# Gather targets of a graph-network kernel: sixteen copies of the prefix rows, and other rows for empty slots

## The reference, cut to what matters

```
h = layernorm(x), clipped at 0
h = h @ W.T + b
_, topk_idx = top_k(adj, 32)           # the lowest index wins among equal values
x = x + max(h[topk_idx], axis=1)
```

## Time and profile before

| | |
|---|---|
| median of three runs | 3695.63 us (3692.3 to 3698.97) |
| span of the profiled execution | 3738.5 us |
| TensorE, VectorE, GpSimd, ScalarE busy | 90%, 70%, 69%, 43% |
| the chain that ended last | TensorE 65%, VectorE 21%, issue 5%, GpSimd 4% |
| GpSimd products L498 | 1024 of 1307 ns |
| gathers L506 | 980, about 1 us each |

### The profile page before, as it was taken

The page is one execution under the profiler, slowest core; times in us unless marked ns, Lnnn a source line. Parts: engine busy times, 40 slices in busy tenths (PEclk is TensorE's granted clock), DMA queues, the critical chain, the costliest instruction groups (busy, mean ns, idle before and its releaser), DMA issues.

```text
span 3738.5 us, 76487 instructions
## 1 busy us (share of the span) xinstructions
PE 3378.0 (90%) x29444; PEld 3342.4 (89%) x29444; DVE 2622.0 (70%) x5491; ACT 1607.0 (43%) x3554; POOL 2592.6 (69%) x2448
## 2 busy tenths in 40 slices
PE   6999999999999999999999999942899898989894
PEld 6999999999999999999999999942888898989894
DVE  6788888788788788211177664647787878878767
ACT  6777887787787786222122211221111111112114
POOL 3998998998998997000487856647888878777500
PEclk9999999999999999999999999975999999999997
DMA  6999999999999999788888888842788887878781
GB/s 217 397 396 367 388 385 352 386 389 352 386 391 351 384 376 388 276 291 296 290 322 319 299 294 311 293 154 77 269 286 291 300 308 284 295 280 308 259 293 57
DMA packets 401324, 1155.22 MB, mean 309 GB/s; under 512 B 36717, under 2 KB 56110, under 8 KB 401006
## 3 DMA queue, kind: packets, MB, share of 16 engines
q1 hardware_dynamic: 360096, 1082.21, 78.4%
q0 software_dynamic: 31360, 64.29, 5.5%
q10 hardware_dynamic: 9550, 4.69, 0.4%
HBM read 874.19 MB, written 276.86 MB: 308 GB/s over the span
## 4 chain that ended last, share of the span: by engine, by line
PE 65%; DVE 21%; issue 5%; POOL 4%; ACT 2%; DMA 1%; another core or an unknown queue 1%; DVEq 1%; POOLq 0%; SPq 0%; ACTq 0%
PE psU L667 18%; PE psT L751 18%; PE psT L655 9%; PE psT L783 8%; PE psU L751 6%; DVE agg L1684 4%; DVE HT L1680 3%; PE psU L783 3%; DVE D L1473 2%; POOL D L498 2%; POOL D L506 2%; DVE GR L1843 1%; DVE W L1684 1%; DMA adj_turned<-ATS 1%
## 5 line engine op out<-in xcount | busy, mean ns | idle before, releaser
L498 POOL TENSOR_TENSOR D<-D,iota 128x512 f32<-128x512 f32 x1024 | 1307.3, 1307 | 115.9 <-ACT D L910 97.6
L667 PE MATMUL psU<-HB,ATS 128*128 128x129 f32 x8192 | 1007.1, 276 | 28.4 <-ACT ATS L903 26.3
L667 PEld LDWEIGHTS psU<-HB,ATS 128*128 128x128 f32 x8192 | 961.1, 193 | 33.3 <-ACT ATS L903 28.6
L783 PE MATMUL psT<-ATS,PIECES 128*128 128x129 f32 x6144 | 804.7, 281 | 172.7 <-ACT ATS L1069 79.3
L783 PEld LDWEIGHTS psT<-ATS,PIECES 128*128 128x128 f32 x6144 | 751.5, 196 | 186.3 <-issue 143.8
L1473 DVE MAX8 D<-D 128x8 f32<-128x512 f32 x1024 | 644.2, 683 | 259.7 <-POOL D L498 251.9
L751 PE MATMUL psT<-GR,PIECES 128*128 128x129 f32 x6144 | 780.7, 276 | 20.1 <-issue 19.3
L751 PEld LDWEIGHTS psT<-GR,PIECES 128*128 128x128 f32 x6144 | 733.2, 192 | 24.9 <-issue 24.2
L506 POOL DMA_INDIRECT D<-h_table,idx_own x624 | 628.4, 1007 | 170.4 <-issue 150.3
L903 ACT ACTIVATE ATS<-psT 128x512 f32<-128x512 f32 x1024 | 555.9, 596 | 270.4 <-PE psT L655 177.1
L910 ACT ACTIVATE D<-PIECES 128x1024 f32<-128x1024 f32 x512 | 544.1, 1063 | 0.0
(11 more groups left out here) (410 smaller groups left out, 2896.9 us busy)
## 6 DMA issues: line engine op xcount, KB each, us to landing
PIECES<-adj_turned SPq DMA_DIRECT2D x512, 1024.0 KB
PIECES<-in_adj SPq DMA_DIRECT2D x256, 1024.0 KB
adj_turned<-ATS SPq DMA_DIRECT2D x512, 512.0 KB, 8.2
D<-h_table,idx_own POOLq DMA_INDIRECT x624
h_table<-HB ACTq DMA_DIRECT2D x8, 512.0 KB, 6.6
D<-h_table,idx_pool POOLq DMA_INDIRECT x215
out_x<-X SPq DMA_DIRECT2D x3, 1024.0 KB, 5.1
ATS<-h_table,idx_pool POOLq DMA_INDIRECT x117
```

The lines of the kernel that those rows point to most:

```text
L498: pool.tensor_tensor(key, key, iota[:, :], ALU.mult).then_inc(keyed, 1)
L667: last = nc.tensor.matmul(sum4(r), AT[K % NAT][:, b * GROUP + r * P:b * GROUP + (r + 1) * P], HB[:, j, :], start=(j == 0 and r % 2 == 0), ...
L783: last = nc.tensor.matmul(acc(h, r), block_of(slot, b, r), Hc[par][:, jj, :], start=(jj == 0 and opens(r)), stop=(jj == CT - 1 and closes(r)))
```

## The change

- The table begins with 16 copies of the 65 prefix rows, 1040 rows in place of 65 (`COPIES`, `BASE`). One DMA writes them all. Each partition uses the copy of its number divided by 8: `lane[:, 2:3]` holds 65 times that, and it is added wherever k was used.
- An empty own slot repeats the first neighbour of its line of eight (near or far). Only where the row has none there does it hold the prefix row as before.
- An empty shared slot reads row 1039 + 15 times the partition's number for near lists, 1039 + 47 times it for far lists. The mask takes its value out as before.
- VectorE builds `lane[:, 2:3]` ahead of the pass, in 15 comparisons that each add to it. Each pick gets two more instructions, and three of its instructions get one more operand. The steps of a staged list (L1534 to L1551) stay as many.

```diff
+COPIES = 16
+    NEAR_STEP, FAR_STEP = 15, 47
-    table = nc.dram_tensor("h_table", (HEAD + N, P), fp32).ap()
+    BASE = COPIES * HEAD
+    table = nc.dram_tensor("h_table", (BASE + N, P), fp32).ap()
+    heads_v = table[0:BASE, :].rearrange("(c p) f -> p c f", p=HEAD)
...
-            pool.iota(lane[:, :], [[0, 1]], base=0, channel_multiplier=1,
+            pool.iota(lane[:, 0:1], [[0, 1]], base=0, channel_multiplier=NEAR_STEP,
+                      allow_small_or_imprecise_dtypes=True).then_inc(ident_ready, 1)
+            pool.iota(lane[:, 1:2], [[0, 1]], base=0, channel_multiplier=FAR_STEP,
...
-                    nc.scalar.dma_start(table[0:HEAD, :], pfxn[:, :]).then_inc(head_stored, 16)
+                    nc.scalar.dma_start(heads_v, pfxn[:, :].unsqueeze(1).to_broadcast([HEAD, COPIES, P])).then_inc(head_stored, 16)
...
+                lists, fills = [a.rearrange("p r (l k) -> p (r l) k", k=8) for a in (top, topd)]
...
+                pk.mark(v.scalar_tensor_tensor(fills, lists, 0.0, lists[:, :, 0:1].to_broadcast([P, 2 * TPG, 8]),
+                                               ALU.is_equal, ALU.mult))
                 pk.mark(v.tensor_copy(POOLN[:, g, :], pooln[:, 0:NEAR_POOL]))
...
+                pk.mark(v.tensor_tensor(lists, lists, fills, ALU.add))
                 pk.mark(v.tensor_tensor(zcum, zcum, sp[:, 2, :].unsqueeze(2).to_broadcast([P, TPG, PREFIX]), ALU.is_lt))
...
-                pk.mark(v.tensor_copy(IDXN[:, ts, 0], sp[:, 3, :]))
+                pk.mark(v.tensor_scalar(IDXN[:, ts, 0], sp[:, 3, :], lane[:, 2:3], None, ALU.add))
...
-                    pk.mark(v.tensor_tensor(into, topd[:, :, to:to + count],
-                                            sp[:, 3, :].unsqueeze(2).to_broadcast([P, TPG, count]), ALU.add))
+                    pk.mark(v.scalar_tensor_tensor(into, topd[:, :, to:to + count], lane[:, 2:3],
+                                                   sp[:, 3, :].unsqueeze(2).to_broadcast([P, TPG, count]),
+                                                   ALU.add, ALU.add))
...
-                link(v.scalar_tensor_tensor(key, empty, lane[:, 0:1], key, ALU.mult, ALU.add))
+                link(v.scalar_tensor_tensor(key, empty, lane[:, 0:1] if near_list else lane[:, 1:2], key, ALU.mult, ALU.add))
...
             dve.wait_ge(pick_constants, 4)
+            link(v.memset(lane[:, 2:3], 0.0))
+            for k in range(1, COPIES):
+                link(v.scalar_tensor_tensor(lane[:, 2:3], lane[:, 0:1], float(NEAR_STEP * k * (P // COPIES)) - 0.5,
+                                            lane[:, 2:3], ALU.is_gt, ALU.add))
+            link(v.tensor_scalar(lane[:, 2:3], lane[:, 2:3], float(HEAD), None, ALU.mult))
+            link(v.tensor_scalar(row_base, row_base, lane[:, 2:3], None, ALU.add))
             link(v.tensor_copy(basep, cbase))
```

More of the change, by code:

```diff
@@ L109, in build @@
     HEAD = PREFIX + 1
-    table = nc.dram_tensor("h_table", (HEAD + N, P), fp32).ap()
-    near_table = table[0:HEAD + NEAR * PIECE, :]
-    early_table = table[0:HEAD + LATE * SGW, :]
-    table_v = table[HEAD:HEAD + N, :].rearrange("(t p) f -> p t f", p=P)
+    BASE = COPIES * HEAD
+    table = nc.dram_tensor("h_table", (BASE + N, P), fp32).ap()
+    near_table = table[0:BASE + NEAR * PIECE, :]
+    early_table = table[0:BASE + LATE * SGW, :]
+    heads_v = table[0:BASE, :].rearrange("(c p) f -> p c f", p=HEAD)
+    table_v = table[BASE:BASE + N, :].rearrange("(t p) f -> p t f", p=P)
     turned = nc.dram_tensor("adj_turned", (NG, NP, P, 2 * GROUP), fp32).ap()
@@ L185, in build @@
         idle_end = sb("idle_end", [P, 384], u8)
-        lane = sb("lane", [P, 1])
+        lane = sb("lane", [P, 3])
         eps_col = sb("eps_col", [P, 1])
@@ L488, in _ @@
             pool.memset(taken, -7.0).then_inc(pick_constants, 1)
-            pool.iota(row_base, [[STRIDE, TPG]], base=-PREFIX, channel_multiplier=0,
+            pool.iota(row_base, [[STRIDE, TPG]], base=1 - BASE, channel_multiplier=0,
                       allow_small_or_imprecise_dtypes=True).then_inc(pick_constants, 1)
@@ L612, in _ @@
             pe.wait_ge(s_load, LOADS)
-            pe.wait_ge(ident_ready, 4)
+            pe.wait_ge(ident_ready, 5)
             nc.tensor.transpose(psX[:, 0:P], wnat[:, 0, :], ident[:, :])
@@ L1511, in general_form @@
                                 ge.link(v.tensor_copy(fidx_row[:, :], fidx[:, :]))
-                                ge.link(v.tensor_scalar(fidx_row[:, :], fidx_row[:, :], float(HEAD), None, ALU.add))
+                                ge.link(v.tensor_scalar(fidx_row[:, :], fidx_row[:, :], float(BASE), None, ALU.add))
                                 ge.mark(v.tensor_copy(IDXG[:, t, :], fidx_row[:, :].unsqueeze(1)))
@@ L1544, in stage_list @@
                 link(v.scalar_tensor_tensor(at_row, o3, -float(STRIDE), at_row, ALU.mult, ALU.add))
-                mark(v.tensor_scalar(idx_pool[par][:, 0:count], at_row, float(PREFIX), None, ALU.add))
+                mark(v.tensor_scalar(idx_pool[par][:, 0:count], at_row, float(BASE - 1), None, ALU.add))
                 mark(v.tensor_scalar(keep[par][:, 0, 0:count], keep[par][:, 0, 0:count], NOT_HERE, None, ALU.mult))
@@ L1874, in _ @@
             dve.wait_ge(s_load, LOADS)
-            dve.wait_ge(ident_ready, 4)
+            dve.wait_ge(ident_ready, 5)
             dve.wait_ge(extra_constants, 4)
```

## The result

The changed kernel takes 3705.73 us (median of 20 runs, 3695.08 to 3711.51), the one before 3694.07 us (20 runs, 3688.01 to 3705.19, on the same chip). The ratio is 1.0031 with a 95% interval of 1.0024 to 1.0039: the change costs 11.7 us (8.9 to 14.4). The forecast was a sum of +8.5 us, between 3.4 and 14.5.

The account below looks back on a forecast made before the run. TensorE works for 90% of a 3738.5 us span, so only its waits matter. Start 5.1 + picks 3.4 + gathers 0 = 8.5 us, added to the median 3695.63, gives 3704 us; range 3683 to 3714.

Parts of the forecast that it names:

- The start of the pass: Adjacency pass start: eighteen chained VectorE instructions, partly beside GpSimd's products, delay first maxima 6.3 us; TensorE stalls 5.1 us.
- The free start: Rival at the pass's start: comparisons slip between GpSimd's products, costing nothing there; about 3698 us, chance 0.25.
- The picks: Two more two-input VectorE instructions in each pick delay TensorE ahead of its stalls; 3.4 us in all (0.6 to 6.3).
- each later stall grows by about 1 us: Sign in the adjacency pass: three later TensorE stalls longer by about 1 us each, from the new pick instructions.
- The gathers: Gather queue: spreading the row addresses gains between 0 and 32 us of DMA engine time, taken as 0.
- crowding rival: Crowded gather rows also hold up other queues' reads, so spreading gains 16 us or more; 3688 or 3672, chance 0.20.
- dear scattered slots: Rival: shared gathers with rows 15 or 47 apart double their engine time; +17 us, 3721, chance 0.07.
- engine time per MB: Sign in the gather queue: DMA engine time per MB stays as before, within 2%.
- TensorE's idle time in the windows: Sign in the gather windows: the forecast is wrong if this idle time falls by more than 10 us.
- The 1.5% of the earlier trace: Gathers where no load runs: 56% crowded addresses cost 1.5% more engine time per MB than 16%, taken as nothing.

Follow-up runs that it names:

- chain moved: The changed kernel with seventeen of its eighteen VectorE start instructions ahead of the wait for `h0_taken`, where VectorE idles; 3679.14 us, ratio 1.0010 to the kernel before.
- sum in PSUM: The changed kernel with the running sum of its fifteen comparisons in PSUM in place of SBUF; 3676.75 us, ratio 1.0006 to the kernel before.
- the start alone: The kernel before with only the eighteen small VectorE instructions added ahead of piece 0, their result zero; 3681.96 us, ratio 1.0026.
- b0: The kernel before, unchanged, profiled a second time beside the experiments; span 3671.8 us, median of its runs 3671.86 us.
- 16 rows in turn: The kernel before with the empty shared slots on rows 64 to 79 by partition number modulo 16; ratio 0.9993.
- picks alone: The kernel before with only the two new VectorE instructions of each pick added; 3676.78 us, ratio 1.0010.

## Why the prediction was right

**The start of the pass** was forecast as: chain 10.2 us, first maxima 6.3 us later, TensorE's stall 5.1. The maxima begin 11.34 us after `alph` (69.98 - 58.64) where it was 5.15 in the earlier trace rows (63.36 - 58.21), so 6.19 later, and the stall is 5.12 us. Even the split fits: five comparisons take 1.15 to 1.23 us each and the `row_base` instruction 1.02, where I had six comparisons at 0.2 + 1.0. The free start falls; the runs with the chain moved and with the sum in PSUM show that the contention, not the count, makes the price.

**What was missing** in this term is the clock. The stalls of 4.6 to 7.6 us that were looked at are followed by 3.7 to 4.9 us at a granted clock of 0.50, and cost 2 to 2.5 us beyond their own length. I counted only the length. The earlier trace rows holds the hint: the products behind a stall there take twice as long as usual. With it the start is 5.1 + 2.1 = 7.2 us; the start alone measured +9.5, interval 5.9 to 13.2.

**The picks** were put at +3.4 and measured +3.7 alone, but this agreement carries little: the interval is -0.4 to 8.1. The step that each later stall grows by about 1 us is not borne out; the stalls of the changed kernel are those of before. The term is neither shown nor excluded.

**The gathers** at 0 held for the rows that this change moves. Spreading the shared slots gives 1.0004, and the changed kernel without its dear start (chain moved, sum in PSUM) is at 1.0010 and 1.0006 (lower ends 0.9998 and 0.9996), where the crowding rival had a gain of 16 us or more against at most 6.3 for the picks, a ratio below 0.998. The crowding rival and the dear scattered slots both fall; a gain of a few microseconds that the picks take back is not excluded, since the sixteen copies were never run alone. Two signs that I had named decide less than I thought. The engine time per MB moves by more than 2% between profiles without a cause in the rows. TensorE's idle time in the windows of the earlier trace rows went from 5.0 to 8.1 us (1820:1960) and from 31.5 to 24.9 (2700:3000), in all 3.6 us less and so under the 10 that I had set, but `b0`, the same kernel as before, has 10.4 and 16.1 there. And my reason was weaker than it looked. The 1.5% of the earlier trace rows lies within the rounding of its MB, and it compares gathers in which no single row has all 128 partitions, so it could only show that moderate crowding is free. It said nothing on one row for all, which costs 2.4%.

**The sum.** Of the 11.7 us measured the traces show 7.2, the start with its slow clock; where the other 4.5 lie, in the picks or in the noise (8.9 to 14.4 for the whole), is not shown. The parts run alone add to 9.5 + 3.7 + 1.5 = 14.7, but the last two have zero in their intervals. The range of 3683 to 3714 around 3704 held the 3705.73. That the middle came so near is partly luck: the picks' 3.4, which no run shows clear of zero, filled the place of the clock's 2.1, and the 3695.63 that I added to was 1.6 above the median of the 20 runs. No version here is clearly faster than the kernel before: with the sum in PSUM or with the chain moved it comes back to within 0.1% by the ratio (3.7 and 7.3 us between the medians).

## What to carry to other kernels

A chain of tiny dependent instructions is cheap or dear by what runs beside it: seventeen on VectorE held up nothing while GpSimd rested, and the eighteen held up the first maxima by 6 us beside its products; the sum in PSUM or a place a few microseconds earlier gives that back. Price a new TensorE stall of some 5 us or more at its length plus the slow clock behind it, here 2 to 2.5 us. Where many lanes need a row that they will not use, two or more rows taken in turn were enough here, and the spreading of this change bought nothing more that could be measured; one row for all is the thing to avoid.

## What the runs showed of the hardware that I had not expected

- With one 512-byte row for all 128 partitions in the shared gathers' empty slots, the gather queue's engine time goes from 5.9% to 11.1% of the span and the kernel slows by 2.45%; with two rows in turn it is 6.2% and 0.01%. Between two rows and one lies a step; from 128 rows down to two there is no slope.
- The slow clock behind a stall lasted no longer after 7.60 us of standing still (4.4 us) than after 4.59 (4.9 us, the start alone, above). Not every pause brings it: behind one of 2.20 us (chain moved, at 1094) and one of 2.44 (16 rows in turn, at 1364) the next 16 products took 2.05 us at a granted clock of 1.00, behind one of 2.40 (the changed kernel, at 1149) 3.12 us, with the clock falling as they ran. TensorE's timeline with the picks alone, behind the longest:

```profile
621.66 3.81 PE L667 MATMUL psU<-HB,ATS 128*128 128x129 f32 x16 [7.60 <-ACT ATS L903]
```

- One execution of a kernel can be 44 us (1.2%) above its median, as in the earlier trace rows, and 33 above the longest of 20 timed runs, without a longer stall in the adjacency pass (the four take 5.2 to 7.4 us there, 5.5 to 6.2 in `b0`); a second profile of before, on another chip, was within 0.1 us of its median there.
